# Attention with a memory, in front of routed experts: the memory's reads side by side in PSUM, one operation for both quotients, and the result's halves transposed by a DMA

## The chip, the cores and the metric

The kernel runs on one core of a Trainium2 chip. A core has five engines that run side by side, each with its own list of instructions: TensorE (PE) multiplies matrices, VectorE (DVE), ScalarE (ACT) and GpSimd (POOL) work on elements, and SyncE (SP) issues DMAs here. They meet through semaphores alone. TensorE writes to PSUM, eight banks of 128 partitions by 2 KB; GpSimd and the DMAs don't reach PSUM. The metric is the time of one execution on the device in microseconds, lower is better.

## The reference, cut to what matters

One transformer layer on x of 8 x 1024 x 256 in float32: a modulated layer norm, an attention with a compressive memory over segments of 64 tokens (16 heads of 16), a gated residual, a second modulated layer norm, and a mixture of 8 experts with the best 2 for each token.

```
def step(carry, qkv):
    M, z = carry
    q, k, v = qkv
    sq = _sigma(q)                                   # elu + 1
    denom_q = jnp.sum(sq * z[:, :, None, :], axis=-1, keepdims=True) + EPS
    A_mem = jnp.matmul(sq, M) / denom_q
    A_dot = jnp.matmul(jax.nn.softmax(scores, axis=-1), v)
    A_s = beta * A_mem + (1.0 - beta) * A_dot
    sk = _sigma(k)
    denom_k = jnp.sum(sk * z[:, :, None, :], axis=-1, keepdims=True) + EPS
    V_prev = jnp.matmul(sk, M) / denom_k
    M_new = M + jnp.einsum('bhtk,bhtv->bhkv', sk, v - V_prev)
    z_new = z + jnp.sum(sk, axis=-2)
    return ((M_new, z_new), A_s)
```

The attention's result is multiplied by W_o, gated and added to x. Two quotients are taken of the memory: `A_mem` (the queries' read) and `V_prev` (the keys' read).

## The kernel before

The attention works on 64 tiles of 128 tokens: tile t holds segment t // 4 of the two batches 2j and 2j + 1, where j = t % 4 (the segment's number is `s`, the tile's buffer of two is `b`). A tile goes through some 50 small stages, each a function that waits for what it needs and issues its instructions on one engine. Products of float32 precision are made of two halves in float16, a high part and a rest, in three products (`PARTS`).

The table `program` sets the order. For each engine it lists stages with a lag: in round i the engine runs, in the list's order, each stage for tile i minus its lag. Nothing reorders this at run time; an engine that waits holds up all that stands behind it. From round to round each engine repeats the same list, so the time per tile is that of the engine, or of the loop of waits between engines, that is slowest. The stages that matter here, in the way of one tile:

- `proj_qk`, `qk_high`, `q_rest`: the projections and their halves. `stack_high` and `stack_low` (L475) on SyncE bring them by six DMAs into `stk`, behind `qkh` and `qlo`; `stack_high` of t also waits for `sT` of t - 2, since `stk` has two buffers.
- `scores` (L620) waits for all six DMAs; `row_max` (L627) on VectorE waits for `scores`. `scores_by_key` (L652, L656, its end is `sT`) fills banks F and G, `softmax_exp` reads them.
- `sigma` (L607) makes `sig`; `mem_mm` (L682) reads the memory by queries and by keys into the same banks F and G, which `scores_by_key` needs next. For each of two groups g it writes 68 columns asked for by queries (64 of values, 4 of divisors) and 132 by keys (the same and 64 more, by which `sk_act` gets the keys back). In a bank the two groups' 68 columns lie first, then the two groups' 132.
- `mem_den` (L691 twice, L693), `mem_rec` (L697): divisors and their inverse. `mem_a` and `mem_v` (both L699, by the helper `scaled`): the quotients, 128x256 each, to `memA` (four buffers) and `vp` (two buffers). `v_new` (L714) subtracts in `vp`, `update` (L728) multiplies it into the memory's update, `update_add` (L741) adds that on GpSimd.
- `pv` (L752), `pv_dve` (L773): the softmax part, to `att_o`. `a_add` (L781, GpSimd) adds `memA`. `a_high` (L786, ScalarE) and `a_rest` (L790, GpSimd) make the result's halves `ah`. `a_trans` (L796) transposes them in four blocks of 128x128 on TensorE into bank A, `a_act` (L802, ScalarE) copies 128x512 to `aT`, `w_o` (L808) multiplies by W_o.
- `resid` (L814), `res_add` (L817), then the second layer norm, `h2_trans`, `router` and `logit_copy`. `store` (L487) writes the tile's rows, and in rounds of odd segments, four rounds of eight, it also stores two segments to `out` by two DMAs (L495).

In rounds 33 to 80 the engines also load and split the experts' weights between the stages (L75 on ScalarE, L77 on VectorE). After the attention the experts run: gathers, transposing DMAs (`x_trans`, L1288, issued by SyncE: 128x512 halves each), products, and scatters with an add.

Of the kernel before, what the change touches and what calls it, by code (L numbers as in the profile page):

```python
# [41 lines left out]
MI = 132  # L42
KS = SEG + 3 * DK
# [157 lines left out]
def attention(nc, ctx, sb_, sem_, psum, banks, x, cT, wmod, wqT, wkT, wvT, woT, beta, rwT, ident,  # L201
              mem_mask, causal_rows, max_rows, rows_of_batch, routing_constants, out, rows_dram,
              idf, idh, logits, passed, xall, w13s, w13, wqkv, placed, trib, iota, tok_id):
    def sb(name, shape, dt=F32):
        return sb_(name, shape, dt, ctx)
# [19 lines left out]
    vp = sb("vp", [P, 2, G, 2, MW])  # L225
# [15 lines left out]
    asked = bkFG[:, :, 0:G * MW].rearrange("p c (g w) -> p c g w", w=MW)  # L241
    known = bkFG[:, :, G * MW:G * (MW + MI)].rearrange("p c (g w) -> p c g w", w=MI)
# [16 lines left out]
    def set_up_gpsimd(e):  # L259
# [10 lines left out]
        for b_ in range(2):  # L270
            e.memset(vp[:, b_, :, :, SEG:MW], 1.0).then_inc(s_set if b_ else s_c, 1)
# [39 lines left out]
    def set_up_vector(e):  # L311
# [39 lines left out]
        pair = btile2[:, :].rearrange("p (n two) -> p two n", two=2)  # L351
        for par in range(2):
            rows = slice(par * SEG, (par + 1) * SEG)
            e.tensor_scalar(inv_om[rows, :], pair[rows, par, :], 1.0, 1.0 / A_SCALE, ALU.add, ALU.mult).then_inc(s_gb, 1)
        for j in range(1, NJ):
            modulations(j)
    def set_up_tensor(e):
# [7 lines left out]
        for j in range(NJ):  # L365
# [3 lines left out]
            for n in range(3):  # L369
# [20 lines left out]
    dd = sb("dd", [P, 2, 2, 2, G, HQ])  # L390
    memA = sb("memA", [P, 4, D])
# [13 lines left out]
             "sT exp phi plo memm den rec mV mA vpr skt upm umul madd PV pdn rcp ado aadd ahi alo AT aT Wo "  # L405
# [5 lines left out]
    s_st = [sem(f"s_st{j}") for j in range(4)]  # L411
    PER_SEGMENT = ("eps", "pow", "nmr")
    BANK_FREE = {
        "memm": ((("exp", 2),),
             (("mA", 1), ("mV", 1), ("skt", 1),)),
# [10 lines left out]
        "AT": ((("h1T", -5), ("h1L", -5),),  # L426
             (("aT", 1),)),
        "sT": ((("mA", -1), ("mV", -1), ("skt", -1),),
# [3 lines left out]
        "T1": ((("aT", 6),),  # L432
             (("h1T", 1), ("h1L", 1),)),
# [7 lines left out]
    class Tile:  # L441
# [232 lines left out]
    def mem_mm(k):  # L674
# [3 lines left out]
        for g in range(G):  # L678
            for a, (at, width) in enumerate(((g * MW, MW), (G * MW + g * MI, MI))):
# [5 lines left out]
    def mem_den(k):  # L685
        k.wait("memm")
        k.wait("skt")
        k.wait("mA", 2)
        k.wait("mV", 2)
# [787 lines left out]
```

## Time and profile before

| | |
|---|---|
| median of 3 runs | 1295.41 us (1291.19 to 1302.98) |
| the profiled execution | 1294.72 us, of it the span 1292.9 us |
| busy, share of the span: PE, DVE, ACT, POOL | 89%, 70%, 55%, 73% |
| in the chain that ended last | PE 43%, of it L1302 28% and L1336 14% (the experts) |
| DMA, mean over the span | 118 GB/s |

The page cuts the span into 40 slices of 32.3 us, with the busy share of each engine in tenths (9 is 90% or more) and the granted clock of TensorE:

```profile
PE   4689999999999898999623899999999999999995
DVE  3599999999999999999888544445544444445542
ACT  2377888988888888998533233333333333333331
POOL 3168999999999999999922376776666767666653
PEclk8599999999999999999655899999999999999998
```

Slices 3 to 19 are the attention's full rounds, all four engines near full. Slices 20 to 22 are its drain and the routing, with the clock at half. Then come the experts, where TensorE is full. A timeline's row tells the start (us from the span's start), the length, engine, line, operation and tiles; in brackets stands the idle time before it and who ended it. A line with xN merges N instructions, the waits between them included.

### The profile page before, as it was taken

What the parts mean: (1) busy time and instruction counts of PE and PEld (TensorE: products, weight loads), DVE (VectorE), ACT (ScalarE), POOL (GpSimd) and SP (SyncE); (2) the same over time, 40 slices, a digit from 0 to 9 for tenths busy, and PEclk for the clock granted to TensorE, in tenths of its full rate; (3) what the DMA queues carried; (4) which work ended last, traced back from release to release, by engine and by line L of the source; (5) the groups of instructions that cost most, each with busy time, mean ns of one, the idle gap of its engine ahead of it and who ended that gap; (6) DMA issues with size and microseconds to landing.
All of it is one profiled execution on the core that took longest, in us unless ns stands there. A gap on an engine that the chain in (4) does not pass through costs nothing. (4 is left out here: it accounts for less than half of the span.)

```text
span 1292.9 us, 53648 instructions
## 1 busy us (share of the span) xinstructions
PE 1150.3 (89%) x19576; PEld 978.4 (76%) x19576; DVE 911.5 (70%) x2515; ACT 712.0 (55%) x1419; POOL 939.8 (73%) x989
## 2 busy tenths in 40 slices
PE   4689999999999898999623899999999999999995
PEld 1477777888777777777413788888888888888884
DVE  3599999999999999999888544445544444445542
ACT  2377888988888888998533233333333333333331
POOL 3168999999999999999922376776666767666653
PEclk8599999999999999999655899999999999999998
DMA  8323343234333333333355587778687677887860
GB/s 226 78 69 83 95 136 114 89 107 120 104 105 110 108 107 113 102 117 98 103 166 136 119 138 130 135 134 138 127 141 134 133 133 137 133 138 132 137 108 1
DMA packets 201706, 153.09 MB, mean 118 GB/s; under 512 B 101658, under 2 KB 179570, under 8 KB 201330
## 3 DMA queue, kind: packets, MB, share of 16 engines
q0 software_dynamic: 32592, 56.75, 25.6%
q1 hardware_dynamic: 160770, 81.89, 24.3%
q10 hardware_dynamic: 8096, 11.01, 3.3%
q8 instruction: 171, 2.80, 0.9%
q14 instruction: 77, 0.63, 0.2%
HBM read 63.58 MB, written 44.04 MB: 83 GB/s over the span
## 5 line engine op out<-in xcount | busy, mean ns | idle before, releaser
L1302 PE MATMUL psum<-xT,xall 128*128 128x256 f16 x3408 | 386.0, 274 | 15.8 <-DMA xT<-grow 15.4
L1302 PEld LDWEIGHTS psum<-xT,xall 128*128 x3408 | 334.5, 98 | 56.0 <-issue 16.4
L1364 POOL DMA_INDIRECT out<-late,sidx x142 | 229.6, 1617 | 158.5 <-DVE late L1353 109.0
L1310 ACT ACTIVATE sg<-psum 128x512 f32<-128x512 f32 x142 | 84.6, 596 | 283.9 <-PE psum L1302 202.6
L1282 POOL DMA_INDIRECT grow<-moe_rows,gidx x142 | 153.7, 1082 | 86.9 <-DVE gidx L1154 44.0
L1315 DVE SCALAR_TENSOR_TENSOR late<-psum,sg 128x512 f32<-128x512 f32 x142 | 98.1, 691 | 167.9 <-ACT sg L1310 107.7
L1336 PE MATMUL psum<-w2s,hT 128*128 x1704 | 197.7, 273 | 2.4 <-DVE w2s L1390 2.1
L1336 PEld LDWEIGHTS psum<-w2s,hT 128*128 128x128 f16 x1704 | 166.6, 98 | 22.2 <-issue 2.9
L1326 DVE TENSOR_TENSOR hT<-late,hT 128x512 f16<-128x512 f32 x142 | 98.6, 695 | 98.8 <-ACT hT L1322 82.8
L1322 ACT ACTIVATE hT<-late 128x512 f16<-128x512 f32 x142 | 89.4, 630 | 112.3 <-DVE late L1315 100.9
L672 POOL TENSOR_TENSOR pT<-sc,pT 128x1024 f16<-128x1024 f32 x64 | 136.5, 2133 | 10.3 <-ACT pT L668 10.1
L558 PE MATMUL psum<-h1T,wqkv 128*128 128x128 f16 x1536 | 99.3, 223 | 0.9 <-DVE h1T L550 0.9
L558 PEld LDWEIGHTS psum<-h1T,wqkv 128*128 128x128 f16 x1536 | 93.8, 100 | 3.0 <-DVE h1T L550 1.1
L627 DVE TENSOR_REDUCE mx<-psum 128x16 f32<-128x1024 f32 x64 | 77.8, 1216 | 4.9 <-PE psum L620 4.3
L773 DVE TENSOR_TENSOR att_o<-psum,rr 64x128 f32<-64x128 f32 x256 | 73.8, 288 | 4.8
L1353 DVE SCALAR_TENSOR_TENSOR late<-psum,wrow,grow 128x256 f32<-128x256 f32 x142 | 62.0, 478 | 18.4 <-PE psum L1336 18.2
L817 POOL TENSOR_TENSOR xall<-xall,gat 128x256 f32<-128x256 f32 x64 | 47.1, 735 | 35.2 <-DVE gat L814 35.1
L663 ACT ACTIVATE sc<-psum 128x1024 f32<-128x1024 f32 x64 | 65.6, 1025 | 10.0 <-PE psum L656 9.2
L668 ACT ACTIVATE pT<-sc 128x1024 f16<-128x1024 f32 x64 | 67.7, 1057 | 2.0
L682 PE MATMUL psum<-mem,sig 64*64 64x68 f32 (+1 forms) x2048 | 59.9, 255 | 3.4 <-DVE sig L607 3.2
L652 PE MATMUL psum<-stk 112*64 112x64 f16 x2048 | 58.0, 199 | 4.1 <-DVE vp L699 2.3
L808 PE MATMUL psum<-wo,aT 128*128 128x256 f16 x384 | 55.6, 284 | 2.5 <-ACT aT L802 2.5
(263 smaller groups left out, 2286.8 us busy)
## 6 DMA issues: line engine op xcount, KB each, us to landing
stk<-qk SPq DMA_DIRECT2D x384, 64.0 KB, 2.8
moe_rows<-hrows SPq DMA_DIRECT2D x64, 256.0 KB, 3.7
out<-xall SPq DMA_DIRECT2D x64, 128.0 KB, 3.3
raw<-in_w ACTq DMA_DIRECT2D x26, 256.0 KB, 3.5
xall<-in_x ACTq DMA_DIRECT2D x16, 256.0 KB, 4.0
raw<-in_w SPq DMA_DIRECT2D x8, 512.0 KB, 8.7
xall<-in_x SPq DMA_DIRECT2D x8, 384.0 KB, 8.3
grow<-moe_rows,gidx POOLq DMA_INDIRECT x142
```

Of the source, the lines that this page charges most:

```text
L558: i = k.e.matmul(bkB[:, n * P:(n + 1) * P], wqkv[:, b_, c, n * P:(n + 1) * P], h1T[:, k.b, a, c, :], start=(c == 0 and (a, b_) == PARTS[0] ...
L627: done(k.e.tensor_reduce(mx[:, k.b, :], bkDE.rearrange("p h (n k) -> p (h n) k", k=SEG), axis=X, op=ALU.max, negate=True), "mx")
L672: done(k.e.tensor_tensor(pT[:, k.b, 1, :, :].rearrange("p n t -> p (n t)"), sc[:, k.b, :], pT[:, k.b, 0, :, :].rearrange("p n t -> p (n t) ...
L773: i = k.e.tensor_tensor(att_o[b2 * SEG:(b2 + 1) * SEG, k.b, :].rearrange("p (n w) -> p n w", w=2 * DK)[:, :, par * DK:(par + 1) * DK], de[ ...
L1282: k.e.indirect_dma_start(grow[:, k.j, q, :], None, rows_dram, at).then_inc(s_g[k.j], 16)
L1302: i = k.e.matmul(bank[:, n * LONG:(n + 1) * LONG], w13s[:, bass.ds(ex_reg * (G * 4 * I) + ((2 * c + b_) * 2 * I + col), P)], xT[:, k.x, a, ...
L1310: done(k.e.activation(sg[:, half, :], bGate[half][:, :], ACT.Silu, scale=1.0 / W_SCALE), "sg")
L1315: done(k.e.scalar_tensor_tensor(out=hf[:, half, :], in0=bUp[half][:, :], scalar=1.0 / W_SCALE, in1=sg[:, half, :], op0=ALU.mult, op1=ALU.m ...
L1322: done(k.e.activation(h_part(k, half, 0), hf[:, half, :], ACT.Copy), "hhi")
L1326: done(k.e.tensor_tensor(h_part(k, half, 1), hf[:, half, :], h_part(k, half, 0), ALU.subtract), "hlo")
L1336: i = k.e.matmul(bY[k.b][:, q * D:(q + 1) * D], hT[:, k.b, a, n, q * P:(q + 1) * P], w2s[:, b_, bass.ds(ex_reg * (KC * D) + n * D, D)], st ...
L1364: k.e.indirect_dma_start(out_rows, bass.IndirectOffsetOnAxis(ap=sidx[:, n:n + 1], axis=0), yo[:, k.v, q, :], None, bounds_check=B * T - 1, ...
```

## The change

Four things change; what is computed stays.

1. The reads of the memory lie side by side. Each group has 256 columns of its bank, the 68 asked for by queries and right behind them the 132 by keys (`PER_G`), so that the two values of a group stand 68 columns apart and the four groups of both banks 256 apart.
2. `mem_a` and `mem_v` become `mem_av`, one operation of 128x512 into `av` (three buffers, both quotients beside each other). `mem_den` has one `scalar_tensor_tensor` instead of two. `mem_av` waits for the sum `aadd` of three tiles back, where `mem_a` waited for four back; it waits for `upm` of three tiles back, where `mem_v` waited for two. The columns of W_v and the rows of W_o are put in another order on the host, so that a quotient's four blocks are in the order of the banks.
3. `a_trans` and `a_act` go. `a_turn` on SyncE issues one transposing DMA from `ah` to `aT`, behind `alo` of its tile and `Wo` of two tiles back; `w_o` and `a_high` wait for its landing.
4. The lags: `a_turn` has 7 on SyncE, between `stack_high` (3) and `store`; `w_o` has 7 instead of 6, and all behind it (`resid`, the second layer norm, `h2_trans`, `router`, `store`, `logit_copy`) one more than before.

```
-    asked = bkFG[:, :, 0:G * MW].rearrange("p c (g w) -> p c g w", w=MW)
-    known = bkFG[:, :, G * MW:G * (MW + MI)].rearrange("p c (g w) -> p c g w", w=MI)
+    reads = bkFG.rearrange("p c (g w) -> p (c g) w", w=PER_G)
+    found = reads[:, :, 0:2 * MW].rearrange("p n (a w) -> p n a w", w=MW)
...
+        def turned(self, back=0):
+            if self.t >= back:
+                self.e.wait_ge(s_aT[self.b], 16 * ((self.t - back) // 2 + 1))
...
-        for hh in range(2):
-            k.e.scalar_tensor_tensor(out=dd[:, k.b, 0, hh, :, :], in0=asked[:, hh, :, SEG:MW], scalar=W_SCALE * EPS_MEM,
-                                     in1=inv_beta[:, hh, :, :], op0=ALU.add, op1=ALU.mult)
-        done(k.e.tensor_scalar(dd[:, k.b, 1, :, :, :], known[:, :, :, SEG:MW], W_SCALE * EPS_MEM, None, ALU.add), "den")
+        k.e.scalar_tensor_tensor(out=dd[:, k.b, :, 0, :], in0=found[:, :, 0, SEG:MW], scalar=W_SCALE * EPS_MEM,
+                                 in1=inv_beta[:, :, :, :].rearrange("p c g f -> p (c g) f"), op0=ALU.add, op1=ALU.mult)
+        done(k.e.tensor_scalar(dd[:, k.b, :, 1, :], found[:, :, 1, SEG:MW], W_SCALE * EPS_MEM, None, ALU.add), "den")
...
-    def mem_v(k):
+    def mem_av(k):
         k.wait("rec")
-        k.wait("upm", 2)
-        done(scaled(k, vp[:, k.b, :, :, 0:SEG], 1, known), "mV")
-    def mem_a(k):
-        k.wait("rec")
-        k.wait("aadd", 4)
-        done(scaled(k, memA[:, k.j, :].rearrange("p (g c w) -> p g c w", g=G, c=2), 0, asked), "mA")
+        k.wait("upm", 3)
+        k.wait("aadd", 3)
+        done(k.e.tensor_tensor(av[:, k.t % 3, :, :, 0:SEG].rearrange("p n a (f d) -> p n a f d", d=DK),
+                               found[:, :, :, 0:SEG].rearrange("p n a (f d) -> p n a f d", d=DK),
+                               dd[:, k.b, :, :, :].unsqueeze(4).to_broadcast([P, 2 * G, 2, HQ, DK]), ALU.mult), "mAV")
...
-        done(k.e.tensor_tensor(att_o[:, k.b, :], att_o[:, k.b, :], memA[:, k.j, :], ALU.add), "aadd")
+        whole = att_o[:, k.b, :].rearrange("p (n w) -> p n w", w=SEG)
+        done(k.e.tensor_tensor(whole, whole, by_feature(k, 0), ALU.add), "aadd")
...
-    def a_trans(k):
...
-    def a_act(k):
...
+    def a_turn(k):
+        k.wait_apart(("alo",))
+        k.wait_apart(("Wo", 2))
+        k.e.dma_start_transpose(aT[:, k.b, :, :, :].rearrange("p a c t -> p (a c) t"),
+                                ah[:, k.b, :, :].rearrange("p a d -> p (a d)")).then_inc(s_aT[k.b], 16)
     def w_o(k):
-        k.wait("aT")
+        k.turned()
...
-        "sync": [(4, stack_low), (3, stack_high), (13, store)],
+        "sync": [(4, stack_low), (3, stack_high), (7, a_turn), (14, store)],
```

SyncE's queue, in the middle of the attention, before: the two DMAs of `stack_high` of one tile, the store, then the four of `stack_low`.

```order
L495 DMA out<-xall 64x2x256 x2
L475 DMA stk<-qk 16x4x512 x2
L475 DMA stk<-qk 16x8x256 x4
L487 DMA moe_rows<-hrows 128x512
L495 DMA out<-xall 64x2x256 x2
L475 DMA stk<-qk 16x4x512 x2
L475 DMA stk<-qk 16x8x256 x4
```

And after. `DMA_TRANSPOSE` now stands behind each `stack_high`; the stores and the next `stack_low` are one place further back, in rounds with stores to `out` (L497) and without.

```order
L497 DMA out<-xall 64x2x256 x2
L477 DMA stk<-qk 16x4x512 x2
L477 DMA stk<-qk 16x8x256 x4
L792 DMA_TRANSPOSE aT<-ah 128x4x128
L489 DMA moe_rows<-hrows 128x512
L477 DMA stk<-qk 16x4x512 x2
L477 DMA stk<-qk 16x8x256 x4
L792 DMA_TRANSPOSE aT<-ah 128x4x128
```

VectorE, the part with divisors and quotients, before: `dd` are the divisors, `memA` and `vp` the quotients.

```order
L691 SCALAR_TENSOR_TENSOR dd<-psum,inv_beta 128x8 x2
L693 TENSOR_SCALAR dd<-psum 128x16
L641 SCALAR_TENSOR_TENSOR mTs<-psum,mTs 16x128
L824 BN_AGGR mv<-bst 128x2
L697 RECIPROCAL dd<-dd 128x32
L828 TENSOR_SCALAR rstd<-mv 128x1
L77 SCALAR_TENSOR_TENSOR xall<-raw,xall 128x336
L506 BN_AGGR mv<-bst 128x2
L699 TENSOR_TENSOR memA<-psum,dd 128x2x2x64
L699 TENSOR_TENSOR vp<-psum,dd 128x2x2x64
L503 BN_STATS bst<-xall 128x6
```

And after. One of the L691 and one of the quotients are gone; nothing else has another neighbour.

```order
L691 SCALAR_TENSOR_TENSOR dd<-psum,inv_beta 128x4x4
L693 TENSOR_SCALAR dd<-psum 128x4x4
L643 SCALAR_TENSOR_TENSOR mTs<-psum,mTs 16x128
L815 BN_AGGR mv<-bst 128x2
L697 RECIPROCAL dd<-dd 128x32
L819 TENSOR_SCALAR rstd<-mv 128x1
L78 SCALAR_TENSOR_TENSOR xall<-raw,xall 128x336
L508 BN_AGGR mv<-bst 128x2
L702 TENSOR_TENSOR av<-psum,dd 128x8x64
L505 BN_STATS bst<-xall 128x6
```

TensorE, from `pv` to `w_o`, before: L796 are the transposes.

```order
L752 MATMUL psum<-vs,pT 128x33 x48
L796 MATMUL psum<-idh,ah 128x128 x4
L652 MATMUL psum<-stk 64x64 x16
L656 MATMUL psum<-mTs,sel 128x128 x4
L652 MATMUL psum<-stk 64x64 x16
L656 MATMUL psum<-mTs,sel 128x128 x4
L808 MATMUL psum<-wo,aT 128x256 x6
```

And after, where `pv` is followed by `scores_by_key` at once.

```order
L749 MATMUL psum<-vs,pT 128x33 x48
L654 MATMUL psum<-stk 64x64 x16
L658 MATMUL psum<-mTs,sel 128x128 x4
L654 MATMUL psum<-stk 64x64 x16
L658 MATMUL psum<-mTs,sel 128x128 x4
L799 MATMUL psum<-wo,aT 128x256 x6
```

## Rows read from the trace of the kernel before

**Rows 1.** Busy time in two stretches of the attention: window, length, engines, clock, DMA.

```profile
212.00:338.00 126.00, 122.47 (x3258) 102.62 (x3254) 121.49 (x391) 112.99 (x244) 121.17 (x154) 1.00 0.35 104
341.00:618.00 277.00, 252.82 (x6716) 211.46 (x6714) 266.75 (x830) 242.92 (x520) 257.37 (x314) 1.00 0.36 108
```

**Rows 2.** Timeline of TensorE (PE), one round from score product to score product.

```profile
258.25 0.69 PE L620 MATMUL psum<-stk 112*64 112x64 f16 x32
...
263.79 0.40 PE L796 MATMUL psum<-idh,ah 128*128 128x128 f16 x4
264.11 0.44 PE L652 MATMUL psum<-stk 112*64 112x64 f16 x16
...
265.19 0.40 PE L656 MATMUL psum<-mTs,sel 128*128 128x128 f16 x4
...
266.86 0.70 PE L620 MATMUL psum<-stk 112*64 112x64 f16 x32
```

**Rows 3.** The second stretch, row maximum (L627, one per tile) alone.

```profile
341.00:618.00 277.00, 36.41 (x30) 1.00 0.36 108
```

**Rows 4.** Waits, 212 to 338 us: who waited, for whom, total, times, longest.

```profile
POOL xall L817 <- DVE gat L814: 4.8, 9, 0.7
...
PE psum L728 <- issue: 3.4, 14, 0.4
```

**Rows 5.** Timeline of VectorE (DVE): start, length, instruction; first stretch.

```profile
231.61 0.69 DVE L600 SCALAR_TENSOR_TENSOR qk<-psum,qk 128x512 f16<-128x512 f32 x1
232.22 0.68 DVE L607 SCALAR_TENSOR_TENSOR sig<-psum,ex 128x512 f32<-128x512 f32 x1
...
235.41 0.24 DVE L691 SCALAR_TENSOR_TENSOR dd<-psum,inv_beta 128x8 f32<-128x8 f32 x2
...
235.76 0.28 DVE L641 SCALAR_TENSOR_TENSOR mTs<-psum,mTs 16x128 f16<-16x128 f32 x1
...
236.61 0.42 DVE L699 TENSOR_TENSOR memA<-psum,dd 128x256 f32<-128x256 f32 x1
236.95 0.41 DVE L699 TENSOR_TENSOR vp<-psum,dd 128x256 f32<-128x256 f32 x1
```

**Rows 6.** Timeline of GpSimd (POOL), one row.

```profile
233.02 0.73 POOL L781 TENSOR_TENSOR att_o<-att_o,memA 128x256 f32<-128x256 f32 x1
```

**Rows 7.** Source line 796, the transposes: who they waited for, in all.

```profile
  ACT ah L786: 2.2, 2
```

**Rows 8.** Costliest lines: the copy of the transposed halves on ScalarE (ACT).

```profile
L802 ACT ACTIVATE aT<-psum 128x512 f16<-128x512 f16 x64 | 38.2, 597 | 6.5 <-PE psum L796 6.4
```

**Rows 9.** Source line 1288, the transposing DMAs of the experts: issue time, min/median/max.

```profile
L1288 SPq DMA_TRANSPOSE xT<-grow x142: 1189/1268/2018, 704.9 to 1249.4; - x142
```

**Rows 10.** DMA issues: size and median us from issue to landing.

```profile
stk<-qk SPq DMA_DIRECT2D x384, 64.0 KB, 2.8
```

**Rows 11.** Timelines of SyncE and TensorE around the first of them.

```profile
704.94 9.67 SPq L1288 DMA_TRANSPOSE xT<-grow  x5
...
713.39 0.82 PE L1302 MATMUL psum<-xT,xall 128*128 128x256 f16 x3 [15.39 <-DMA xT<-grow]
```

**Rows 12.** Timeline of SyncE's queue, a round without them.

```profile
276.27 3.11 SPq L475 DMA_DIRECT2D stk<-qk  x4
```

**Rows 13.** Timeline of SyncE's queue (SPq), a round with stores to `out`.

```profile
257.07 1.21 SPq L475 DMA_DIRECT2D stk<-qk  x2
258.40 1.14 SPq L487 DMA_DIRECT2D moe_rows<-hrows  x1
259.58 1.29 SPq L495 DMA_DIRECT2D out<-xall  x2
260.99 3.67 SPq L475 DMA_DIRECT2D stk<-qk  x4
```

**Rows 14.** Timeline of TensorE, the drain of the attention.

```profile
645.89 1.46 PE L808 MATMUL psum<-wo,aT 128*128 128x256 f16 x6 [0.75 <-ACT aT L802]
```

**Rows 15.** Timeline of VectorE, its last wait in the attention.

```profile
655.02 0.52 DVE L77 SCALAR_TENSOR_TENSOR xall<-raw,xall 128x352 f16<-128x352 f32 x1 [1.78 <-ACT xall L75]
```

**Rows 16.** Source line 620, `scores`: what they waited for, in all.

```profile
  DMA stk<-qk: 2.1, 2
```

More of the change, by code:

```diff
@@ L42 @@
 MI = 132
+PER_G = 256
 KS = SEG + 3 * DK
@@ L350, in set_up_vector @@
         e.wait_ge(s_gb, 6)
-        pair = btile2[:, :].rearrange("p (n two) -> p two n", two=2)
+        pair = btile2[:, :].rearrange("p (g c u two) -> p two c g u", g=G, c=2, two=2)
         for par in range(2):
             rows = slice(par * SEG, (par + 1) * SEG)
-            e.tensor_scalar(inv_om[rows, :], pair[rows, par, :], 1.0, 1.0 / A_SCALE, ALU.add, ALU.mult).then_inc(s_gb, 1)
+            e.tensor_scalar(inv_om[rows, :].rearrange("p (c g u) -> p c g u", c=2, g=G), pair[rows, par], 1.0, 1.0 / A_SCALE, ALU.add, ALU.mult).then_inc(s_gb, 1)
         for j in range(1, NJ):
@@ L411, in attention @@
     s_st = [sem(f"s_st{j}") for j in range(4)]
+    s_aT = [sem(f"s_aT{b_}") for b_ in range(2)]
     PER_SEGMENT = ("eps", "pow", "nmr")
@@ L710, in v_new, with by_feature @@
+    def by_feature(k, a):
+        return av[:, k.t % 3, :, a, 0:SEG]
     def v_new(k):
-        k.wait("mV")
+        k.wait("mAV")
         k.wait("vhi")
-        seen = vp[:, k.b, :, :, 0:SEG].rearrange("p g c w -> p (g c) w")
+        seen = by_feature(k, 1)
         done(k.e.scalar_tensor_tensor(out=seen, in0=bkC[:, 0:D].rearrange("p (n w) -> p n w", w=SEG), scalar=1.0 / W_SCALE,
@@ L728, in update @@
                     i = k.e.matmul(bank[lanes, g * MW:(g + 1) * MW], skt[r, k.b, g * P + lanes.start:g * P + lanes.stop],
-                                   vp[r, k.b, g, hh, :], start=True, stop=True)
+                                   av[r, k.t % 3, hh * G + g, 1, :], start=True, stop=True)
         done(i, "upm")
@@ L748, in pv @@
             for gu in range(4):
-                pair = (gu // 2) * 4 + half * 2 + gu % 2
+                pair = half * 4 + gu
                 for a, b_ in PARTS:
@@ L788, in a_rest @@
         k.wait("ahi")
-        k.wait("AT", 2)
+        k.turned(2)
         done(k.e.tensor_tensor(ah[:, k.b, 1, :], att_o[:, k.b, :], ah[:, k.b, 0, :], ALU.subtract), "alo")
-    def a_trans(k):
-        k.wait("ahi")
-        k.wait("alo")
-        k.wait_banks("AT")
-        for n in range(2 * G):
-            i = k.e.transpose(bkAh[:, n * P:(n + 1) * P],
-                              ah[:, k.b, :, :].rearrange("p a d -> p (a d)")[:, n * P:(n + 1) * P], idh[:, :])
-        done(i, "AT")
-    def a_act(k):
-        k.wait("AT")
-        k.wait("Wo", 2)
-        done(k.e.activation(aT[:, k.b, :, :, :].rearrange("p a c t -> p (a c t)"), bkAh[:, 0:2 * D], ACT.Copy), "aT")
+    def a_turn(k):
[3 more added lines that the diff above has]
+                                ah[:, k.b, :, :].rearrange("p a d -> p (a d)")).then_inc(s_aT[k.b], 16)
     def w_o(k):
-        k.wait("aT")
+        k.turned()
         k.wait_banks("Wo")
```

62 lines of the change are left out of this document (27 added, 35 removed).

## The prediction

> **What bounds the kernel now.** I read the profile's page first, then the window sums, the timelines of the engines, the waits, and last the timeline of SyncE's queue. The page's slices show two halves: the attention up to about 670 us, then the experts, where TensorE is busy nearly all the time. The edit touches the attention alone, so the second half is taken as unchanged (about 624 us).
>
> The window sums show how even the attention is [rows 1]. From 212 to 338 us VectorE is busy 121.5 of 126 us (96%), TensorE 122.5, GpSimd 121.2, ScalarE 113.0, all at the full granted clock. From 341 to 618 us VectorE stays at 96% (266.8 of 277) while TensorE falls to 91% and GpSimd to 93%: VectorE there also prepares the experts' weights. One tile takes 8.61 us in the first stretch (score product 258.25 to score product 266.86 [rows 2]) and 277 / 30 = 9.23 us in the second [rows 3].
>
> Who leads? VectorE has no idle gap in either stretch beyond the steps between its instructions. GpSimd waits for VectorE's `gat` (4.8 us in the first stretch [rows 4]), and TensorE stands before the memory update (L728, 3.4 us in 14 rounds [rows 4]), which by the code needs `sig`, a VectorE product. So VectorE sets the round, TensorE follows some 0.2 us behind saturation, GpSimd 0.3 us.
>
> **The change, part by part.**
>
> *VectorE, the quotients.* Two 128x256 operations become one of 128x512. Their printed lengths (0.42 and 0.41) overlap, so I count from start to start: 236.61 to 236.95, 0.34 each, 0.68 for both [rows 5]. The nearest row of 512 columns from PSUM is L600, whose successor starts 0.61 later (231.61 to 232.22) [rows 5]. Saved: 0.07 us. *The divisors:* two L691 and one L693 take 0.35 from 235.41 to L641 at 235.76 [rows 5]; one small operation of three goes, which is a third at most and about 0.07 by the same start-to-start reckoning. Sum 0.14 us per tile; bounds 0.07 (only the quotients) and 0.25 (0.42 + 0.41 less 0.69, plus 0.12, if the printed lengths were what counted). I take 0.14, since the starts show what the engine really spends. Over some 60 full rounds: **-8.4 us**, with -4 and -15 as ends.
>
> The operands of this one operation step through PSUM in blocks of 64 within 256 as they did before in blocks of 68 and 132, so I expect no other rate. Its sum on GpSimd (L781) and the subtraction read `av` in four pieces of 64; they keep their length, and for GpSimd 0.73 [rows 6].
>
> *The new wait of `mem_av` for the sum of three tiles back.* In the row order that sum is L781 of the same round: it ends 233.02 + 0.73 = 233.75, the quotients start at 236.61 [rows 5, 6]. It is done 2.9 us early and costs nothing; if GpSimd fell back by 3 us, it would stop VectorE in every round.
>
> *TensorE.* The four transposes go: L796 starts at 263.79, L652 at 264.11, so 0.32 us per tile [rows 2]. Since TensorE isn't first, this buys no time by itself; it lets TensorE stand 0.3 us earlier against VectorE, and takes away the two rounds in which it waited for ScalarE's `ah` before the transposes, 2.2 us [rows 7]. For those, and for the rounds of 9 us before 212 us in which ScalarE with its loads ran late, I take **-2 us** (0 to -5).
>
> *ScalarE.* The copy to `aT` goes, 597 ns per tile [rows 8]. ScalarE had 10% to spare, so nothing.
>
> *SyncE and the transposing DMA.* The same transfer, 128x512 halves into four blocks, stands in the experts' part: SyncE spends 1.27 us on its issue (median of 142) [rows 9]. When it lands no row tells; the bounds are the 2.8 us of a stacking DMA [rows 10] and, from the first pair under a heavy load of weights, 713.39 less 706.2 (704.94 plus one issue), about 7.2 us [rows 11]. The Trainium skill ("VectorE: DVE Perf Modes", section "The three transpose paths") speaks against this edit: it gives TensorE 390 ns for a 128x128 block and the DMA 1309 ns, and advises TensorE where PSUM will do. By that, four blocks would be 5.2 us of transfer, an estimate from that page; the trace's bounds hold it. Either value is covered. The transposing DMA of tile t goes out some 3 us after the scores by key of tile t + 2 (behind `stack_high` of t + 4, which they release), and `w_o` of t stands right behind those of t + 4, two rounds later: 17 - 3 = 14 us for a transfer of 2.8 to 7.2.
>
> What is not covered is the issue on SyncE's queue. It stands between `stack_high` and the store, so the store, the two stores to `out` and `stack_low` of the next round all come 1.27 + 0.1 = 1.4 us later. Whether that hurts is read where `scores` waits for `stack_low`. In a round without stores to `out`, the four issues end at 276.27 + 3.11 = 279.38 [rows 12]; the last began about 0.6 before and lands 2.8 later [rows 10], at 281.6, and the score product is due at 266.86 + 2 x 8.61 = 284.1 [rows 2]: 2.5 us of slack, enough. In a round with them, the four end at 264.66 [rows 13], the last lands at 266.6 to 266.9, and the product started at 266.86 [rows 2]: slack 0.0 to 0.3. This is a tight one, its issues took 3.67 us where 3.11 and less occur; for the mean of such rounds I take 0.7. Half of all rounds are of this kind. Against 1.4 stand this slack and the 0.3 by which TensorE now reaches the trigger of `stack_high` earlier, so a product comes some 0.4 us late in the 16 such rounds of the first half. Since the next round's trigger shifts with it, about half of this is lost: 16 x 0.2 = 3 us. In the second stretch VectorE's longer round gives another 0.6 us and I count 1 us. Sum **+4 us** (0 to +19).
>
> *The drain.* Everything behind `w_o` is one round later, so one more drain round follows, about 5 us. In it and in the four rounds ahead `w_o` no longer waits for the four transposes (0.6 at half clock) and the copy (0.75 [rows 14]): about 1.3 us each, 5 in all; and VectorE's last wait of 1.78 us for ScalarE [rows 15] should shrink, as ScalarE's part of the pipeline is a tile further back. I take **0** (-3 to +4).
>
> Sum: -8.4 - 2 + 4 + 0 = -6.4. The profiled execution took 1294.7 us (span 1292.9), 0.7 below the median of 1295.4, so the runs should show 1288.3 to 1289. **I forecast 1289 us.** The runs of before spread over 12 us, so 1% is about what can be told from no change.
>
> **The rivals.**
>
> *The stacks decide (slower).* Place: `scores` behind `stack_low` in the rounds with stores to `out`. If the transposing DMA also holds up the DMAs behind it in the queue for as long as its issue, their landing moves by 2.7 us instead of 1.4. In the first half's 16 rounds that is 2.7 - 1.0 = 1.7 late, between half lost (14) and all lost (27); with 2 to 4 more in the second half and -10.4 gained, 1301 to 1316. It decides from a lateness of 0.65 us per such round (10.4 / 16). For it: the slack of 0.0 to 0.3 [rows 13]. Against it: `scores` waited for a stack twice in all of before, 2.1 us [rows 16], though stores of 256 KB stood ahead. Chance 0.22.
>
> *More than VectorE's share comes back.* If the engines limit each other by jitter, not by VectorE's sum, relief on TensorE (0.32), ScalarE (0.6) and VectorE (0.14) shortens the round by up to 0.32: 60 x 0.3 = 18 us, 1274 to 1282. For it: three engines at 96%. Against it: GpSimd loses no work and is at 121.2 of 126, which allows 0.33 in the first stretch. Chance 0.18.
>
> *Nothing moves.* The merged operation costs as much as the two, or GpSimd, itself near full, takes up the gain: 1292 to 1297. Chance 0.1.
>
> *The forecast*, 1283 to 1296, has 0.5.
>
> **How the numbers follow.** 1278 to 1304 leaves out half of the two outer cases, 0.2. Faster by over 1% is below 1282.5: most of the second rival and an edge of the forecast, 0.2. Slower by over 1% is above 1308: less than half of the first rival, 0.09. The rest, 0.71, is within 1%.
>
> **What would show it.** The merged operation near 0.69 us and its successor 0.61 behind it; the round maximum to round maximum 8.45 to 8.5 in the first stretch and about 9.1 in the second; VectorE still at 96%, TensorE near 95% in the first; no wait of `w_o` for the transposed tile; `scores` with new waits for `stk<-qk` in the rounds with stores to `out`, summing to some 4 to 8 us of idle TensorE. The forecast is wrong if these waits pass 15 us, if the merged operation takes over 0.83 us, if VectorE waits for GpSimd, or if the granted clock falls below full in the attention as TensorE does less.

## The result

| | before | changed |
|---|---|---|
| median | 1296.62 us (1291.19 to 1302.98, 4 runs) | 1308.46 us (1302.03 to 1310.82, 4 runs) |
| the profiled execution | 1294.72 us, span 1292.9 | 1302.03 us, span 1299.5 |
| ratio | | 1.008, 95% interval 1.0042 to 1.0119 |

The changed kernel is slower, by about 10 us (0.8% of 1297), where 1289 us was forecast with 1278 to 1304. The median lies in the range of the rival "the stacks decide". The profiled execution is the fastest of the changed kernel's four, 6.4 us below their median, so its rows show less of the loss than the medians do.

The window sums of the changed kernel, the same two stretches as [rows 1] (window, its length, busy time of PE, PEld, DVE, ACT, POOL, granted clock, DMA share, GB/s):

```profile
212.00:338.00 126.00, 115.82 (x3059) 97.33 (x3059) 113.93 (x346) 100.95 (x219) 114.89 (x145) 0.97 0.46 114
341.00:618.00 277.00, 246.44 (x6593) 206.55 (x6596) 262.13 (x767) 228.90 (x492) 256.77 (x314) 1.00 0.48 122
```

In the first stretch no engine is near full any more: VectorE has 113.9 of 126 us (90%) where [rows 1] has 121.5. The DMA engines are busy for 0.46 of the time instead of 0.35. The waits of the whole execution (total, times, longest) say who stood for whom:

```profile
PE psum L622 <- DMA stk<-qk: 21.6, 19, 1.8
DVE mx L629 <- PE psum L622: 17.2, 21, 1.6
```

The score product (L622, L620 before) waits 21.6 us for the stacks. Before, the same view of TensorE's products had 1.0 us (the 2.1 of [rows 16] counts the weight loads as well). VectorE's row maximum then waits for that product, 17.2 us instead of 4.3. TensorE's timeline in one such round:

```profile
253.20 0.40 PE L658 MATMUL psum<-mTs,sel 128*128 128x128 f16 x4
...
256.40 0.69 PE L622 MATMUL psum<-stk 112*64 112x64 f16 x32 [1.46 <-DMA stk<-qk]
...
266.22 0.84 PE L622 MATMUL psum<-stk 112*64 112x64 f16 x32 [1.59 <-DMA stk<-qk]
```

From product to product 9.82 us where [rows 2] has 8.61, and both times TensorE stands idle before it. What follows such waits can cost nearly as much. Four rounds from product to product, this one and the next three (window, its length, TensorE's busy time, granted clock, DMA share, GB/s):

```profile
256.40:266.22 9.82, 8.14 (x221) 1.00 0.42 117
266.22:275.63 9.41, 9.36 (x219) 0.82 0.38 102
275.63:285.59 9.96, 8.13 (x221) 1.00 0.46 125
285.59:295.30 9.71, 9.67 (x221) 0.82 0.41 95
```

The first and the third end in a wait for the stacks. The second and the fourth end in none: TensorE is busy all the time there, but for part of it at the lower of its two levels (a granted clock of 0.50 from 267 to 269.5 us, and again from 287.5 to 290), and the same 220 or so instructions keep it busy for 9.4 to 9.7 us instead of 8.1. SyncE's queue at the time of the first wait (three timeline cuts: the low stack of one tile, the high stack of the next, and what stands behind it, up to the stores to `out`):

```profile
251.73 2.52 SPq L477 DMA_DIRECT2D stk<-qk  x4
254.79 2.16 SPq L477 DMA_DIRECT2D stk<-qk  x2
257.13 1.24 SPq L792 DMA_TRANSPOSE aT<-ah  x1
258.49 0.51 SPq L489 DMA_DIRECT2D moe_rows<-hrows  x1
259.05 1.32 SPq L497 DMA_DIRECT2D out<-xall  x2
```

The scores by key that release `stack_high` end at 253.20 + 0.40 = 253.6, but the queue comes to it at 254.79 only. In the kernel before, [rows 13] begins with the same two issues at 257.07, and TensorE's timeline shows their release right ahead:

```profile
256.58 0.40 PE L656 MATMUL psum<-mTs,sel 128*128 128x128 f16 x4
```

There the queue was waiting when the release came (256.98), and issued 0.1 us later. This is the difference between an issue that is 1.4 us later once and a queue that no longer gets empty: in the changed kernel the lateness is taken into the next round. How often SyncE still came first and waited for the scores by key, from 212 to 338 us, before and after (total, times, longest):

```profile
SPq L69 <- PE psum L656: 25.0, 15, 1.8
```

```profile
SPq L70 <- PE psum L658: 12.2, 9, 1.7
```

Before, it waited for this release in each of some 15 rounds, 1.7 us on average; in the changed kernel in 9.

The row maximum's starts answer to it. Seven rounds with stores to `out` among them took 60.5 us in the kernel before (224.5 to 285.0), 8.64 each, and 64.5 us in the changed one (221.8 to 286.3), 9.21 each. Over all 64 tiles the first and the last row maximum lie 563.2 us apart before and 569.7 after:

```profile
L627 DVE TENSOR_REDUCE mx<-psum x64: 1211/1214/1226, 58.8 to 622.0; 128x16 f32<-128x1024 f32 x64
```

```profile
L629 DVE TENSOR_REDUCE mx<-psum x64: 1215/1216/1226, 57.2 to 626.9; 128x16 f32<-128x1024 f32 x64
```

The quotients did what they should. VectorE's timeline:

```profile
232.56 0.17 DVE L691 SCALAR_TENSOR_TENSOR dd<-psum,inv_beta 128x16 f32<-128x16 f32 x1
232.65 0.17 DVE L693 TENSOR_SCALAR dd<-psum 128x16 f32<-128x16 f32 x1
232.84 0.28 DVE L643 SCALAR_TENSOR_TENSOR mTs<-psum,mTs 16x128 f16<-16x128 f32 x1
...
233.72 0.69 DVE L702 TENSOR_TENSOR av<-psum,dd 128x512 f32<-128x512 f32 x1
234.33 0.42 DVE L505 BATCH_NORM_STATS2 bst<-xall 128x6 f32<-128x256 f32 x1
```

The divisors take 232.56 to 232.84, 0.28 us where [rows 5] has 0.35; the merged quotients 0.61 where the two had 0.68.

The transposing DMA in the trace of the changed kernel (its issue on SyncE and its landing, min/median/max):

```profile
L792 SPq DMA_TRANSPOSE aT<-ah x64: 1202/1226/2933, 80.6 to 646.7; - x64
...
DMA to landing us min/median/max: 2.4/3.5/5.6
```

### The profile page after: what moved, and what is told of

Same layout as the page of the kernel before. It is cut to its first block and busy times, and to the rows that moved or that the text cites. A ratio compares the mean times of both kernels' runs of the same rounds, so it can differ in the third digit from the quotient of the medians.

```text
span 1299.5 us, 52812 instructions
## 1 busy us (share of the span) xinstructions
PE 1135.0 (87%) x19320; PEld 966.5 (74%) x19320; DVE 902.3 (69%) x2387; ACT 684.3 (53%) x1355; POOL 929.3 (72%) x990
## 5 line engine op out<-in xcount | busy, mean ns | idle before, releaser
L1354 POOL DMA_INDIRECT out<-late,sidx x142 | 226.8, 1598 | 168.6 <-DVE late L1343 103.7
L1272 POOL DMA_INDIRECT grow<-moe_rows,gidx x142 | 145.4, 1024 | 85.6 <-issue 43.0
L629 DVE TENSOR_REDUCE mx<-psum 128x16 f32<-128x1024 f32 x64 | 78.0, 1219 | 17.4 <-PE psum L622 17.2
L654 PE MATMUL psum<-stk 112*64 112x64 f16 x2048 | 58.6, 199 | 7.0 <-issue 4.5
L622 PE MATMUL psum<-stk 112*64 112x64 f16 x2048 | 45.0, 198 | 21.8 <-DMA stk<-qk 21.6
```

What stands on the lines that cost most here:

```text
L629: done(k.e.tensor_reduce(mx[:, k.b, :], bkDE.rearrange("p h (n k) -> p (h n) k", k=SEG), axis=X, op=ALU.max, negate=True), "mx")
L1272: k.e.indirect_dma_start(grow[:, k.j, q, :], None, rows_dram, at).then_inc(s_g[k.j], 16)
L1354: k.e.indirect_dma_start(out_rows, bass.IndirectOffsetOnAxis(ap=sidx[:, n:n + 1], axis=0), yo[:, k.v, q, :], None, bounds_check=B * T - 1, ...
```

## The experiments

All times are medians beside runs of the kernel before on the same chip; the ratio is to these, with its 95% interval. The other columns come from one profiled execution of each kernel: what the score product (TensorE's products alone) waits for the stacks; the granted clock from 80 to 600 us; "rounds", the time from the first to the last row maximum; "tail", from the start of the last difference of `ah` (`a_rest`) to the start of the last single product of `w_o`; and "to experts", from the last row maximum to the first product of the experts (L1302 before), that is, what of the drain and the routing reaches the second half.

| kernel | median us | ratio | waits for stk | clock | rounds | tail | to experts |
|---|---|---|---|---|---|---|---|
| before | 1295.9 to 1297.1 | 1 | 1.0 | 1.00 | 563.2 | 5.8 | 91.4 |
| changed | 1308.46 | 1.008 (1.0042 to 1.0119) | 21.6 | 0.99 | 569.7 | 10.4 | 94.0 |
| merged_only | 1291.69 | 0.9966 (0.9943 to 0.9989) | 0.7 | 1.00 | 558.8 | 5.9 | 91.3 |
| turn_only | 1309.04 | 1.0096 (1.0069 to 1.0122) | 17.2 | 0.97 | 576.9 | 10.4 | 93.5 |
| turn_act | 1292.27 | 0.9966 (0.9943 to 0.9989) | 1.9 | 1.00 | 559.9 | 10.4 | 93.5 |
| turn_early | 1297.6 | 0.9989 (0.9964 to 1.0014) | 4.8 | 0.99 | 560.7 | 10.4 | 93.8 |
| tiny2 | 1303.41 | 1.0058 (1.0036 to 1.008) | 15.9 | 0.99 | 572.4 | 5.9 | 90.8 |
| out_act | 1291.85 | 0.996 (0.994 to 0.998) | 2.9 | 1.00 | 552.1 | 10.4 | 93.8 |
| lags_only | 1299.41 | 1.0025 (1.001 to 1.0041) | 1.2 | 1.00 | 565.8 | 10.3 | 92.6 |
| old_lags | 1305.47 | 1.0069 (1.0045 to 1.0093) | 20.3 | 0.99 | 570.9 | 5.4 | 91.3 |
| turn_act_now | 1334.87 | 1.0301 (1.0273 to 1.0329) | none | 0.97 | 605.6 | 5.4 | 91.9 |
| out_act_old_lags | 1292.35 | 0.9972 (0.9946 to 0.9997) | 1.3 | 1.00 | 556.4 | 5.4 | 91.3 |
| merged_out_act | 1293.25 | 0.9971 (0.995 to 0.9993) | none | 1.00 | 560.8 | 5.8 | 90.8 |

The question was where the gain went and where 10 us came from. Theory Q: SyncE's issue time. Its rival T: the traffic of the transposing DMA (the DMA share rose by 0.11). Theory D: the later round of `w_o` is paid in the drain.

### Each half of the change alone

**merged_only** is the changed kernel with `a_trans`, `a_act`, their waits and all lags of before put back; of its edit, cut:

```diff
-        "sync": [(4, stack_low), (3, stack_high), (7, a_turn), (14, store)],
+        "sync": [(4, stack_low), (3, stack_high), (13, store)],
-... (4, pv), (3, scores_by_key), (7, w_o), ...
+... (4, pv), (6, a_trans), (3, scores_by_key), (6, w_o), ...
+... (10, a_high), (11, a_act), ...
```

> The reads of the memory side by side, one operation for the quotients, one divisor operation fewer and the new order of the features, with the transposes on TensorE, the copy on ScalarE and the old lags. Theory (the gain of VectorE is real but smaller than forecast): undisturbed rounds 0.09 us shorter in the first stretch and 0.06 in the second as in the changed kernel, some 4 to 5 us in all, 1290 to 1292 beside 1296 before; scores wait for the stacks as rarely as before (2 to 4 us). Rival (the layout itself costs, since the quotients' operation steps through two banks): 1296 or more.

Measured: 0.9966, 4.4 us less (interval 1 to 7), and in the profiled executions the rounds are 558.8 us against 563.2. The layout and its one operation are a gain, about half of what the forecast took. For why only half, the first stretch gives a reading:

```profile
212.00:338.00 126.00, 123.62 (x3252) 103.31 (x3250) 121.26 (x364) 112.75 (x244) 121.65 (x154) 1.00 0.36 108
```

```profile
PE psum L723 <- issue: 0.9, 5, 0.2
```

TensorE is at 123.6 of 126 (98%), and its waits before the memory update (now L723) fell from 3.4 us in 14 rounds [rows 4] to 0.9 in 5. The row maximum waited for TensorE in 15 rounds where it did in 10. So once VectorE was 0.14 us shorter, TensorE may have led in part of the rounds: the 0.2 us by which it had stood behind. This is argued and not shown. GpSimd is as near, at 121.7 of 126 us in this kernel, and no kernel here relieves it; and relieving TensorE on top of the merged quotients gained nothing that can be measured (the last section of the experiments).

**turn_only** is the kernel before with the other half: `a_turn`, the waits for it, and the later lags.

> The transposing DMA and its lags alone, with the two quotient operations of before. Both theories of the DMA expect the loss here: 1308 plus the 4 to 5 us that the quotients no longer give, 1310 to 1315, and 18 to 24 us of waits of the score product for the stacks. If instead the new order of PSUM were at fault, this kernel would be at 1296.

Measured: 1.0096, 12.4 us more (interval 9 to 16), with 17.2 us of waits. That is 1309.0, 1 us below the expected range. The loss sits in this half alone. The sum of the halves, -4.4 + 12.4 = 8.0, agrees with the 10 of the whole within the intervals. The 17.2 us fell just short of the 18 expected.

### Issue time or traffic

**turn_act**: the same DMA, issued by ScalarE.

```diff
-        "sync": [(4, stack_low), (3, stack_high), (7, a_turn), (14, store)],
+        "sync": [(4, stack_low), (3, stack_high), (14, store)],
-        "scalar": [..., (10, a_high), (0, var_eps), ...
+        "scalar": [..., (10, a_high), (11, a_turn), (0, var_eps), ...
```

> The changed kernel with the transposing DMA issued by ScalarE, in the place where the copy of the transposes stood, so that SyncE's queue is the one of before and the traffic is that of the changed kernel. Theory Q (SyncE's issue time is what costs): waits of the score product for the stacks fall from 21.6 to about 2 to 5 us, rounds with stores to out from 9.5 to 10.2 back to about 8.8, time 1286 to 1293. Rival T (the transposing DMA's traffic slows the transfers of the stacks): waits stay at 15 us or more, time 1303 to 1310. Rival A (1.2 us of issue on ScalarE makes ScalarE the bound: 101 + 14 x 1.2 = 118 of 126 us): waits gone, yet no faster than 1300.

```profile
212.00:338.00 126.00, 117.50 (x3165) 99.01 (x3163) 120.29 (x364) 106.47 (x230) 122.20 (x155) 1.00 0.46 122
```

```profile
PE psum L622 <- DMA stk<-qk: 1.9, 4, 1.0
```

The DMA share is that of the changed kernel, 0.46, and the bytes per second are more, 122 against 114. The waits for the stacks are gone, and the time is 15 us below the changed kernel by the ratios (16 by the medians). The stacking DMAs land in 2.9 us (median) where they took 2.8 [rows 10]. The traffic is there and does no harm that shows: T falls.

**tiny2** is the counterpart: the kernel before, with SyncE's time and no traffic.

```diff
+    def small(k):
+        for n in range(2):
+            k.e.dma_start(tiny[:, k.t, n, :], idh[:, 0:2]).then_inc(e_w8, 16)
-        "sync": [(4, stack_low), (3, stack_high), (13, store)],
+        "sync": [(4, stack_low), (3, stack_high), (7, small), (13, store)],
```

> The kernel before with two small DMAs (128 x 4 bytes each) put into SyncE's queue where the transposing DMA stands in the changed kernel: its issue time without its traffic (two issues of about 0.5 to 0.6 us, 1.1 us and the steps between). Theory Q: waits of the score product for the stacks rise from 2 to 12 us or more, time 1302 to 1308, DMA traffic as before (0.36). Rival T: waits and time as before, 1296 to 1298.

```profile
L488 SPq DMA_DIRECT2D tiny<-idh x128: 465/603/1944, 78.7 to 636.8; - x128
```

```profile
212.00:338.00 126.00, 119.43 (x3087) 99.93 (x3078) 115.42 (x376) 106.22 (x231) 115.41 (x146) 0.97 0.35 101
```

```profile
PE psum L624 <- DMA stk<-qk: 15.9, 15, 2.2
```

Two issues of 0.60 us each, a DMA share as before (0.35), 15.9 us of waits and 6.5 us more time (7.5 by the ratio; interval 5 to 10). These 6.5 and the later round (2.5 by lags_only, below) make 9 of the 12.4 of turn_only. Q holds from both sides: traffic without SyncE's time costs nothing that shows, SyncE's time without traffic costs.

The clock belongs to this path. In the table it is at 0.97 to 0.99 in the four kernels with over 15 us of these waits, and at 1.00 in those with less than 4, except turn_act_now, where TensorE stood for other reasons (below). In tiny2, 1% of 520 us is some 5 us of TensorE's work, in turn_only 3% are 16 us (estimates from the rounded clocks). How the loss divides into waits and clock isn't measured, since no kernel has the one without the other.

The Trainium skill ("DMA: Bandwidth & Descriptors", section "Issuing engines are not separate DMA queues") says that starting DMAs on several engines saves only the sequencer's time to initiate them, "which is usually small relative to the DMA itself". The first part agrees with turn_act: what was saved was SyncE's time. Small it isn't here, 1.23 us beside a landing of 3.5, and it was the time on the sequencer that decided.

**out_act**: the changed kernel, its transposing DMA left on SyncE, the other issues of the crowded rounds taken off.

```diff
+    def store_out(k):
         if k.s % OUT_SEGS < OUT_SEGS - 1:
             return
+        k.wait_apart(("res",))
-        "scalar": [(6, qk_high), ...
+        "scalar": [(16, store_out), (6, qk_high), ...
```

> The changed kernel, transposing DMA on SyncE as it is, with the stores to out taken off SyncE and issued by ScalarE. Theory Q (the sum of the issues on SyncE in rounds with stores to out): SyncE loses 2.3 to 2.5 us per such round, waits of the score product for the stacks 2 to 5 us, 1291 to 1297. Rival T (traffic of the transposing DMA): waits 15 us or more, 1303 to 1310. ScalarE takes 2.4 us in half of the rounds, 101 + 17 = 118 of 126 us at most, and may itself cost 1 to 3 us.

Measured: 0.996, waits 2.9 us, as expected under Q. The two stores to `out` were the other part of the crowd: with either them or the transposing DMA off SyncE's queue the loss is gone. ScalarE had room for them.

**turn_early**: the same DMA in the same queue, at another place.

```diff
-        "sync": [(4, stack_low), (3, stack_high), (7, a_turn), (14, store)],
+        "sync": [(4, stack_low), (8, a_turn), (3, stack_high), (14, store)],
```

> The changed kernel with the transposing DMA one place earlier in SyncE's row order, ahead of the first stacking DMAs and for the tile before, so that it goes out in the time in which SyncE waits for the scores by key. Theory Q: in rounds without stores to out it fills a gap; in those with them SyncE is busy without a gap (its issues sum to about 8.5 to 10 us of a round), so the sum of the queue decides and only a part comes back: waits 10 to 20 us, 1298 to 1306. If only the place in the queue mattered, waits would fall to 5 us and the time to 1290. Rival T: no change, 1308.

Here the expectation was wrong. I had reckoned that a queue without a gap keeps its sum whatever the order; the waits fell to 4.8 us and the rounds to 560.7. SyncE's timeline in a round with stores to `out` shows why:

```profile
250.67 1.22 SPq L792 DMA_TRANSPOSE aT<-ah  x1
252.44 1.24 SPq L477 DMA_DIRECT2D stk<-qk  x2
253.79 0.53 SPq L489 DMA_DIRECT2D moe_rows<-hrows  x1
254.37 2.30 SPq L497 DMA_DIRECT2D out<-xall  x2
256.78 2.52 SPq L477 DMA_DIRECT2D stk<-qk  x4
```

The transposing DMA now goes out in the time in which SyncE would stand before `stack_high`, which waits for the scores by key, and it ends at 251.89, with a gap of 0.55 left. What counts is what stands between that release and the last stacking DMA, not the sum alone. Why the median, 1297.6, isn't as low as turn_act's although the profiled rounds differ by 0.8 us only, stays open.

### The later round

**lags_only**: the kernel before, transposes and copy kept, everything from `w_o` on one round later.

```diff
-... (11, h2_trans), ... (6, w_o), ... (12, router)
+... (12, h2_trans), ... (7, w_o), ... (13, router)
```

(and one more for each stage behind them on the other engines, `store` among them)

> The kernel before with nothing changed but the lags of everything from w_o on (one round later, as in the changed kernel); transposes and copy stay on TensorE and ScalarE. Theory D (the drain pays for the later round, no matter who transposes): full rounds as before, and from the last difference of a to the last w_o about 10 us instead of 5.6; time 1299 to 1302 beside 1297 (+4 us). Rival (the later round is free, and the 4 us behind the last round maximum of the changed kernel come from the transposing DMA): 1296 to 1298.

Measured: 1.0025 (1.3 to 5.3 us), tail 10.3 instead of 5.8. **old_lags** is the reverse: the changed kernel with the lags of before.

```diff
-        "tensor": [..., (12, h2_trans), ..., (7, w_o), ..., (13, router)],
+        "tensor": [..., (11, h2_trans), ..., (6, w_o), ..., (12, router)],
-        "sync": [(4, stack_low), (3, stack_high), (7, a_turn), (14, store)],
+        "sync": [(4, stack_low), (3, stack_high), (7, a_turn), (13, store)],
```

> The changed kernel, transposing DMA on SyncE where it is, with w_o and all behind it back at the lags of before. Theory D (the later round is what the drain pays for, and it isn't needed: w_o of before starts 8 us after the last difference of a, the DMA needs 1.2 to issue and 3.5 to land): 4 us less than the changed kernel, 1303 to 1306, waits of the score product for the stacks as in the changed kernel (15 to 22 us). Rival (the later round is needed): w_o waits for the transposed tile in the rounds in which SyncE is late, 10 us or more of such waits, 1308 or more.

Measured: 1305.5, ratio 1.0069 against 1.008, tail 5.4, waits for the stacks 20.3 as expected, and no wait of `w_o` for the transposed tile. The medians differ by 3 us in the expected direction (1.4 by the ratios), but the intervals overlap; the tail is what shows the step. In the changed kernel, the last difference on GpSimd and the last two groups of `w_o` on TensorE:

```profile
645.83 0.66 POOL L788 TENSOR_TENSOR ah<-att_o,ah 128x256 f16<-128x256 f32 x1
...
650.20 1.44 PE L799 MATMUL psum<-wo,aT 128*128 128x256 f16 x6 [0.73 <-issue]
...
655.21 1.44 PE L799 MATMUL psum<-wo,aT 128*128 128x256 f16 x6 [0.73 <-issue]
```

and with the old lags:

```profile
646.06 0.66 POOL L788 TENSOR_TENSOR ah<-att_o,ah 128x256 f16<-128x256 f32 x1
...
650.43 1.44 PE L799 MATMUL psum<-wo,aT 128*128 128x256 f16 x6 [0.73 <-issue]
```

From start to start of these rows 9.4 us against 4.4: one drain round of 5.0 us, and the group of `w_o` between is that of the tile before. (The column "tail" goes to the last single product, 1 us behind its group's start.) The drain rounds themselves stayed 5 us long without transposes and copy. The six kernels with the later lags have tails of 10.3 to 10.4, the others 5.4 to 5.9.

But the tail isn't what the execution pays. In the column "to experts" the later lags cost 1.2 us (lags_only against before) to 2.7 us (changed against old_lags), and not 4.5 to 5. VectorE's rows show one reason. [rows 15] has its last wait in the attention, 1.78 us for ScalarE; all seven kernels with the lags of before have it, at 1.78. In the changed kernel, and in the other five with the later lags, 0.30 to 0.31 are left:

```profile
661.73 0.71 DVE L78 SCALAR_TENSOR_TENSOR xall<-raw,xall 128x352 f16<-128x352 f32 x1 [0.31 <-ACT xall L76]
```

So theory D is right in kind and about half as large as the tail says.

**turn_act_now**: `a_turn` on ScalarE so early that `w_o` can keep its old round (all lags are those of before, and SyncE's list is too).

```diff
+        "scalar": [..., (8, p_high), (10, a_turn), (5, h1t), ...
```

> The changed kernel with the transposing DMA on ScalarE's queue, issued one round earlier in ScalarE's rows (behind the high half of the weights of the softmax), and w_o with all behind it at the lags of before. Theory D and Q together: no waits for the stacks (2 to 4 us), and the end behind the last round maximum back to 38 to 39 us from 43: 4 us less than the version with the old place on ScalarE, 1286 to 1290. Against it: ScalarE waits there for GpSimd's a_rest of the same round and holds up its own line (h1t, max_high), or w_o waits for the landing (3 us); then 1292 or more, with new waits of ScalarE.

1334.9, far outside of what I expected. ScalarE's waits and its timeline:

```profile
ACT h1T L547 <- issue: 63.0, 58, 2.2
```

```profile
275.26 1.06 ACT L670 ACTIVATE pT<-sc 128x1024 f16<-128x1024 f32 x1
275.42 1.81 ACTq L792 DMA_TRANSPOSE aT<-ah  x1
277.42 0.38 ACT L547 ACTIVATE h1T<-psum 128x256 f16<-128x256 f32 x1 [1.11 <-issue]
```

`h1t` waits 1.1 us in 58 rounds for the issue ahead of it in its own queue. In turn_act the same issue stood elsewhere:

```profile
274.63 1.22 ACTq L792 DMA_TRANSPOSE aT<-ah  x1
274.77 0.59 ACT L581 ACTIVATE rel<-psum 128x512 f32<-128x512 f32 x1
275.24 0.42 ACT L784 ACTIVATE ah<-att_o 128x256 f16<-128x256 f32 x1
275.95 0.72 ACT L585 ACTIVATE ex<-rel,ln_w 128x512 f32<-128x512 f32 x1 [0.29 <-issue]
```

It runs beside two operations that ScalarE still has ahead of it, and 0.29 us of its 1.22 show in this round (22.4 us in 45 rounds over the execution, 0.5 each, by ScalarE's waits). ScalarE is busy for 106.5 of 126 us in turn_act, some 1.3 us to spare per round; there the first place is dear, and the second costs nothing that shows. That 1.1 us of ScalarE per round make 42 us of rounds (605.6 against 563.2) isn't broken down further; the clock, at 0.97 without any wait for the stacks, may have a part in it, and the DMA landed in 5.4 us here (median) instead of 3.0.

### Both repairs, and what the transposing DMA is worth by itself

**out_act_old_lags** joins the edits of out_act and old_lags; **merged_out_act** is merged_only with the stores to `out` on ScalarE, that is, the same but for the transposing DMA.

> Both repairs together: stores to out issued by ScalarE, and w_o at the lags of before. Theories Q and D: 4 us less than with the stores moved alone (1291.9), 1286 to 1290, with at most 3 us of waits of w_o for the transposed tile and 5 us of the score product for the stacks. Rival: waits of w_o eat the 4 us, 1291 to 1295.

> The merged quotients with transposes on TensorE and the copy on ScalarE, and the stores to out on ScalarE: the same as both repairs together but for the transposing DMA, so the two tell what that DMA gives by itself. If relief of TensorE (0.32 us) and ScalarE (0.6 us) is worth nothing in full rounds: within 1 us of the kernel with both repairs. If it is worth the 2 us of the forecast: this one 2 us slower. ScalarE would have 113 + 17 = 130 of 126 us if the issues were spent in full on it; then this kernel would be at 1300 or more.

0.9972 and 0.9971: equal, so the transposing DMA, with the queue cleared for it and with TensorE down to 118.3 from 123.1 us of 126, gives nothing that can be measured. The two intervals together leave room for some 4 us either way, and the profiled rounds (556.4 against 560.8) would allow a gain of that size. The 4 us that I expected of the old lags on top of out_act didn't show (0.9972 against 0.996): to the experts they gave back 2.5 us (91.3 against 93.8), and out_act's profiled rounds were 4.3 us shorter, for which I have no cause. merged_out_act didn't lose by ScalarE's issues either, against my bound of 1300. Five kernels, merged_only, turn_act, out_act, out_act_old_lags and merged_out_act, beat both the kernel before (by 3.6 to 5.2 us) and the changed one, and can't be told apart by these runs; merged_only is the simplest of them.

## Point by point

**VectorE sets the round** held for the kernel before, with TensorE and GpSimd nearer than thought. **The quotients and the divisors**: saved 0.07 and 0.07 us from start to start, as reckoned. As time it gave 4.4 us (1 to 7) instead of 8.4; the interval reaches close to both. The term "0.14 us per tile over some 60 rounds" took VectorE's saving to come back whole. [rows 1] had TensorE at 122.5 and GpSimd at 121.2 of 126 us; which of the two took the other half isn't shown.

**The reads' new layout, the wait of `mem_av` for the sum of three tiles back**: no cost, as said.

**Transposes and copy gone**, taken for -2: no gain that a pair of kernels shows (out_act_old_lags against merged_out_act, to within some 4 us).

**The transposing DMA itself**: issue 1.23 us (1.27 forecast), landing 3.5 us (median), inside the bounds of 2.8 and 7.2, never waited for. The 5.2 us that I estimated by the page "VectorE: DVE Perf Modes" of the Trainium skill, section "The three transpose paths", lie above the median and inside the range of 2.4 to 5.6. The advice to take TensorE's path where PSUM will do (same page, section "Rules for kernel authors") fits the result here, since the DMA was faster in no pair of kernels. What made it slower, where it was, wasn't the transfer's time but its issue on a queue that was needed.

**SyncE's issue delays the stacks**: the step that failed. The place was right: `scores` behind `stack_low`, mostly in rounds with stores to `out`; so were the 1.4 us (257.13 to 258.49). The mean slack of 0.7 no row measures. The step "a product comes some 0.4 us late ... about half of this is lost: 16 x 0.2 = 3 us" took each round by itself. It left out that 1.4 us use up the gap in which SyncE waited for its release (from 264.66 to the next release in [rows 13]), so that `stack_high` starts 1.2 us late too and the delay is handed on through a series of such rounds. Measured: waits of 21.6 us in 19 rounds, 1.1 each, instead of 4 to 8 in all; 6.5 us of time for the issue time alone (tiny2), and 15 us between the changed kernel and turn_act, where the term had +4 (0 to +19). The rival "the stacks decide" named this place and 1301 to 1316, but by another mechanism (landings held up by the DMA ahead); turn_act and tiny2 show the issue time to be enough. That the time lies in this rival's range is therefore luck as far as its mechanism goes.

**The clock** was named as a sign of being wrong, but stood in no term. It fell to 0.97 in the first stretch, and two of the rounds shown above are some 1 us longer by it, without a wait of their own.

**The drain at 0**: the size was off, within its own bounds of -3 to +4. Between the last row maximum and the experts' first product the changed kernel has 2.6 us more than before (94.0 against 91.4). Of the two things set against the drain round of 5 us, one came true, VectorE's last wait (1.78 us, then 0.31). The other, 1.3 us in each of five drain rounds, didn't, since `w_o` there waited for other things (0.73 us, shown as issue, where it had waited 0.75 for the copy [rows 14]).

Sum by the runs: -4.4 for the quotients, +2.6 for the drain, and for SyncE's queue between +6.5 (tiny2) and +15 (turn_act), together 5 to 13 us; the measured 10 lies between, and the runs don't make it narrower. The profiled rounds alone give 6.5 + 4.4 = 10.9 for the queue. The term's own span of 0 to +19 held this price; the range of the sum ended at 1304 because the upper part of that span was left to a rival with a chance of 0.22. Of the four signs of being wrong two came: the waits passed 15 us, and the clock fell below full.

## What to carry to other kernels

- A queue that issues DMAs is an engine: add up its issues between the event that releases one and the DMA that is waited for, and look whether it is idle when the release comes. As long as it is, a delay is felt once; when it isn't, it is handed on. And where TensorE is made to stand, look at the granted clock of the round after: the wait may not be all that it costs.
- An issue costs by its place in the row: in a stretch in which the engine would wait anyway, or behind work that it still has in hand, it cost little here (turn_early, turn_act); ahead of an operation that others wait for it cost nearly its full length in each round (turn_act_now).
- Where other engines are within 2% of the first, don't count its saving whole: half came back here. And price a pipeline that is made one round deeper at the point where the next phase starts: of a drain round of 5 us, 1.2 to 2.7 arrived there.

## What the runs showed of the hardware

- SyncE spends 0.60 us (median) on issuing a DMA of 128 x 4 bytes, as for a stacking DMA of 64 KB (four in 2.52 us); the store of 256 KB takes 0.51 (258.49). Size was no measure of issue time here.
- A transposing DMA of 128 x 512 halves takes 1.23 us to issue on SyncE and on ScalarE alike, and lands in 3.5 us from SyncE (3.0 from ScalarE in turn_act) with the DMA engines busy for 0.46 of the time. In turn_act_now the same DMA, from ScalarE at another place, landed in 5.4 us at 0.50.
- The granted clock was 1.00 in the first stretch where TensorE's waits for the stacks were short (busy 117.5 to 123.6 of 126 us), and 0.97 in the changed kernel and in tiny2 (115.8 and 119.4 us), where it stood still for over 1 us in several rounds; turn_only and old_lags had 0.99 (115.0 and 115.7). The busy shares of the groups overlap, so what decides isn't shown. In the changed kernel the clock was down in 266.22 to 275.63, behind idle gaps of 1.46 and 1.59 us, and again behind one of 1.41; four waits of 0.68 to 1.26 us in a row, from 331 to 359 us, passed without a fall.
- At the lower clock a round costs more even though TensorE never waits in it: 9.41 and 9.71 us at a mean of 0.82, where [rows 2] has 8.61 at 1.00.
